# Modulated and low-rank feed-forward stages issued from one block instead of two

## The reference, cut to what matters

```python
# _L3_xattn_ref, its second half (the "modulated" stage)
scale_out, shift_out = jnp.split(c_t @ W_film_out + b_film_out, 2, axis=-1)
y = y * (1.0 + mod_gate * scale_out) + mod_gate * shift_out
xt = x_text + y
h = layernorm(xt, g_ffn, b_ffn)
h = jax.nn.gelu(h @ W1 + b1, approximate=False) @ W2 + b2      # 256 -> 1024 -> 256
xt = xt + h
return layernorm(xt, g_norm_out, b_norm_out)

# _L3_ffn_ref (the "low-rank" stage)
P = jnp.einsum('bsd,dr->bsr', x, U1)                           # 256 -> 64
H = jax.nn.gelu(jnp.einsum('bsr,rf->bsf', P, V1) + b1)         # 64 -> 1024
Q = jnp.einsum('bsf,fr->bsr', H, U2)                           # 1024 -> 64
return jnp.einsum('bsr,rd->bsd', Q, V2) + b2                   # 64 -> 256

x = x + _L3_xattn_ref(_layernorm(x, axis=-1), ...)
x = x + _L3_ffn_ref(_layernorm(x, axis=-1), ...)
```

## Time and profile before

| what | value |
|---|---|
| median of 3 runs (lowest to highest) | 4894.45 us (4890.16 to 4894.87) |
| the profiled execution's own time | 4895.16 us |
| its span, first to last instruction | 4893.4 us |
| mean granted TensorE clock, share of full | 0.962 |
| PE busy | 4476.2 us (91%) |
| DVE busy | 3200.3 us (65%) |
| ACT busy | 2002.0 us (41%) |
| POOL busy | 1820.1 us (37%) |

### The profile page before, as it was taken

How to read it: one execution, slowest core, us unless ns; L and a number is a source line. 1 busy time by engine, 2 the same in 40 slices (tenths; PEclk the granted TensorE clock), 3 DMA queues, 4 the chain that set the end, 5 groups by cost and what they waited for, 6 DMA issues and landing times. The chain is left out here.

```text
span 4893.4 us, 90645 instructions
## 1 busy us (share of the span) xinstructions
PE 4476.2 (91%) x31852; PEld 3480.9 (71%) x31852; DVE 3200.3 (65%) x9752; ACT 2002.0 (41%) x4152; POOL 1820.1 (37%) x2248
## 2 busy tenths in 40 slices
PE   7999869999995999699996999999999887999979
PEld 5666547778884888567765788888888645777856
DVE  5888789987552331278872888888888833444344
ACT  3555347754442331155552434434433342222234
POOL 2222145642553331255440333333333304665523
PEclk9999989999997999899998999999999988999989
DMA  4666512245313222222212010011100082222233
GB/s 115 155 154 150 122 60 78 71 139 157 58 55 68 71 70 70 59 72 68 76 52 79 27 28 28 29 31 33 28 28 24 18 277 96 88 85 85 73 114 106
DMA packets 332894, 391.33 MB, mean 80 GB/s; under 512 B 66485, under 2 KB 301467, under 8 KB 321691
## 3 DMA queue, kind: packets, MB, share of 16 engines
q1 hardware_dynamic: 319130, 360.28, 25.9%
q0 software_dynamic: 13312, 25.25, 2.1%
HBM read 296.33 MB, written 89.10 MB: 79 GB/s over the span
## 5 line engine op out<-in xcount | busy, mean ns | idle before, releaser
L2693 PE MATMUL fa_h<-fa_xnT,fa_w 128*128 128x256 f32 x2048 | 484.8, 382 | 0.0
L2705 PE MATMUL fa_y<-fa_w,fa_hT 128*128 128x256 f32 x2048 | 462.5, 379 | 0.0
L2693 PEld LDWEIGHTS fa_h<-fa_xnT,fa_w 128*128 128x128 f32 x2048 | 379.9, 190 | 81.9 <-issue 27.5
L2705 PEld LDWEIGHTS fa_y<-fa_w,fa_hT 128*128 128x128 f32 x2048 | 386.7, 190 | 65.1 <-issue 15.4
L2568 ACT ACTIVATE fa_hT<-fa_h,fa_b 128x256 f32<-128x256 f32 x512 | 214.5, 469 | 533.7 <-PE fa_h L2693 472.3
L516 DVE TENSOR_REDUCE a_mx<-a_score 128x16 f32<-128x1920 f32 x128 | 276.0, 2157 | 53.8 <-PE a_score L700 53.8
L3086 ACT ACTIVATE m_hT<-m_h,m_b 128x256 f32<-128x256 f32 x256 | 107.3, 470 | 363.2 <-PE m_h L3147 363.2
L1700 PE MATMUL r_h<-r_xnT,r_rw 128*128 128x256 f32 x1024 | 246.9, 389 | 0.0
L2007 ACT ACTIVATE e_hT<-e_h,e_b 128x256 f32<-128x256 f32 x256 | 107.3, 470 | 335.4 <-PE e_h L2061 335.4
L1846 POOL DMA_INDIRECT e_xg<-moe_rows,e_idx x64 | 128.6, 2009 | 307.9 <-issue 262.4
L3147 PE MATMUL m_h<-m_hnT,m_w 128*128 128x256 f32 x1024 | 235.7, 379 | 2.5 <-ACT m_hnT L3076 2.5
(11 more groups left out here) (463 smaller groups left out, 10842.1 us busy)
## 6 DMA issues: line engine op xcount, KB each, us to landing
a_floor<-a_lowest SPq DMA_DIRECT2D x64, 960.0 KB, 8.5
cv_toep<-kernels SPq DMA_DIRECT2D x16, 2048.0 KB, 9.3
x<-a_xo SPq DMA_DIRECT2D x96, 256.0 KB, 4.2
f_xb<-x SPq DMA_DIRECT2D x64, 256.0 KB, 2.8
f_xres<-x SPq DMA_DIRECT2D x64, 256.0 KB, 2.9
a_xb<-x SPq DMA_DIRECT2D x64, 256.0 KB, 3.3
e_w<-in_L_ffn_ew SPq DMA_DIRECT2D x16, 1024.0 KB, 7.5
a_cb<-in_ctx SPq DMA_DIRECT2D x96, 90.0 KB, 2.6
```

The costliest lines, as they stand in the source:

```text
L2693: last = pe.matmul(h_ps[j % 2][:, c, :], w1[:, e, k, f:f + P], xnT[it.p][:, k, :], start=k == 0, stop=k == KD - 1)
L2705: last = pe.matmul(bank[:, t * D:(t + 1) * D], hT[e % 2][:, k, t * P:(t + 1) * P], w2[:, e, k, :], start=k == 0, stop=k == KE - 1)
```

## The change

The two stages are put in one block. Each function now returns lists of steps (`Program`) in place of running them, and the new `modulated_to_low_rank` runs both with `run_parts`: the modulated part starts at slot 0, the low-rank part at slot 32. So the slots 32 to 40 hold the last batches of the one and the first of the other. The steps, their lags and their order within a part stay as they were.

What is new beside the form:
- The low-rank part's SP list begins 16 slots early (`-EARLY`), which puts its weight transfers at slot 16 of the modulated part. Its first load of `x` is issued in slot 31.
- `load` waits for the modulated store of the same batch.
- `f_hT` (the 1024-wide hidden values, two buffers) lies in the first eight batches of `xin`, which the modulated part has read by then; the first two batches' gelu waits for `mixed`.
- The PSUM banks are shared. The first use of each by the low-rank part waits for the last use by the modulated part (`values`, `film`, `turned`, `hidden`, `summed`).
- There is one `end_all` for both stages, behind the last store of the program. It clears 67 semaphores. Before, 40 were cleared between the stages and 28 at the end.

```diff
-def modulated_feed_forward(nc, const, src, dst, xin, rows_text, at_all, ctx, w):
+def modulated_feed_forward(nc, const, src, dst, xin, rows_text, at_all, ctx, w, first, area):
...
-    st = Stage(nc, "m3", [const["apart"]])
+    st = Stage(nc, "m3", [const["apart"]], area)
...
-            pipeline(pe, B, DEPTH, [(6, up(0)), (2, film_values), (6, up(1)), (6, up(2)), (2, film_product), (6, up(3)), (5, turn_x), (7, down)])
-    st.end()
+        return Program([(6, up(0)), (2, film_values), (6, up(1)), (6, up(2)), (2, film_product), (6, up(3)), (5, turn_x), (7, down)], 2, start)
+    after = dict(values=(v_ready, B), film=(film_ready, 2 * B), turned=(hn_ready, B), hidden=(h_ready, KH * B), summed=(summed, SUM * B),
+                 mixed=(mixed, MIX * B), stored=stored)
+    return st, after, Part(first, B, DEPTH, sync, gpsimd, vector, scalar, tensor)
...
-    st = Stage(nc, "f3", [const["apart"]])
+    st = Stage(nc, "f3", area=area)
...
-    hT = [st.sb(f"hT{p}", [P, KH, S]) for p in two]
-    t_ps, p_ps, q_ps, y_ps = st.ps("t", [P, 512]), st.ps("p", [P, 512]), st.ps("q", [P, 512]), st.ps("y", [P, TL, D])
-    h_ps = [[st.ps(f"h{m}{half}", [P, 2, S]) for half in range(HALVES)] for m in range(QUADS)]
+    hT = [xin[:, 4 * p:4 * p + 4].rearrange("p b t d -> p (b t d)").rearrange("p (k s) -> p k s", s=S) for p in two]
+    h01, y_ps, p_ps, q_ps, h00, h10, h11, t_ps = (st.ps(n, [P, 512] if n in "tpq" else [P, 2, S]) for n in ("h01", "y", "p", "q", "h00", "h10", "h11", "t"))
+    h_ps = [[h00, h01], [h10, h11]]
...
+    EARLY = 16
...
+            sp.wait_ge(before["stored"][it.p], 16 * (it.h + 1))
             sp.dma_start(xb[it.at][:], src_v[it.i]).then_inc(x_in[it.at], 16)
...
-            load(It(0, 0, 0, B, 4))
-            pipeline(sp, B, DEPTH, [(-1, load), (4, load_residual), (7, store)], **FOUR)
+        return Program([(-1, load), (4, load_residual), (7, store)], 4, start, -EARLY, finish)
...
+                if it.i < 2 and m == 0:
+                    act.wait_ge(*before["mixed"])
...
+            if it.i == 0:
+                pe.wait_ge(*before["values"])
...
+                if it.i == 0 and m == 0:
+                    pe.wait_ge(*before["film"])
+                    pe.wait_ge(*before["turned"])
+                if it.i == 0 and m == 1:
+                    pe.wait_ge(*before["hidden"])
...
+            if it.i == 0:
+                pe.wait_ge(*before["summed"])
...
+def modulated_to_low_rank(nc, const, src, dst, out, xin, rows_text, at_all, ctx, wm, wl):
+    area = Area((nc.sbuf_base, SBUF_END))
+    m3, m3_after, modulated = modulated_feed_forward(nc, const, src, dst, xin, rows_text, at_all, ctx, wm, 0, area)
+    f3, low_rank = low_rank_feed_forward(nc, const, dst, out, wl, xin, B, area, m3_after)
+    run_parts(nc, [modulated, low_rank])
+    end_all(nc, [m3, f3])
```

More of the change, by code:

```diff
@@ L2943, in keep_xt @@
[L2943 to L2967, removed]
+        def load(it):
+            if it.reused():
+                sp.wait_ge(xn_ready, it.i - 1)
+            apart(sp, const)
+            sp.dma_start(xb[it.p][:], src_v[it.i]).then_inc(x_in[it.p], 16)
@@ L2970, in _, with gpsimd, start @@
                 sp.wait_ge(xt_out[p], 16 * (B // 2))
-        @block.gpsimd
-        def _(pool):
+        return Program([(0, load), (1, load_context), (4, keep_xt), (6, load_xt), (7, load_residual), (9, store)], 2, start, finish=finish)
+    def gpsimd(pool):
+        def start():
             pool.wait_ge(weights, 192)
[L2976 to L3011, removed]
@@ new lines, in end @@
+        def end(it):
+            p = it.p
+            c = Chain(pool, ended, it.i, END)
+            pool.wait_ge(xn3_ready, it.i + 1)
+            if it.reused():
+                pool.wait_ge(stored[p], 16 * it.h)
+            c.add(pool.tensor_tensor(xo[p][:], xs[p][:], over(gout), ALU.mult))
+            c.wait()
+            c.add(pool.tensor_tensor(xo[p][:], xo[p][:], over(bout), ALU.add))
+            c.wait()
+            pool.wait_ge(r_in[p], 16 * (it.h + 1))
+            c.add(pool.tensor_tensor(xo[p][:], xo[p][:], xres[p][:], ALU.add))
@@ L3020, in _ @@
             dve.wait_ge(wready, 2)
[L3022 to L3068, removed]
-            act.wait_ge(weights, 192)
[L3071 to L3083, removed]
-                    for c in range(2):
-                        f = 2 * m + c
-                        act.activation(hT[it.p][:, f, :], h_ps[m % 2][:, c, :], ACT.Gelu, bias=b1[:, f:f + 1]).then_inc(h_ready, 1)
-                return step
-            def values_out(it):
-                act.wait_ge(v_done, it.i + 1)
-                if it.reused(1):
-                    act.wait_ge(f_done, it.i)
-                act.copy(vf[:], v_ps[0:SK, :]).then_inc(v_ready, 1)
@@ new lines, in norm_stats, with norm, film_out @@
+        def norm_stats(it):
+            dve.wait_ge(x_in[it.p], 16 * (it.h + 1))
+            layer_norm_stats(dve, Chain(dve, stats, it.i, 4), xb[it.p], stt[it.p], mv[it.p], const)
+        def norm(it):
+            dve.wait_ge(roots, 2 * it.i + 2)
+            if it.reused():
+                dve.wait_ge(mixed, MIX * (it.i - 1))
+            normalise(dve, xb[it.p], mv[it.p], rs[it.p], xn[it.p])[-1].then_inc(xn_ready, 1)
+        def film_out(it):
+            dve.wait_ge(f_done, it.i + 1)
+            if it.reused():
+                dve.wait_ge(mixed, MIX * (it.i - 1))
+            for t in range(TL):
+                dve.scalar_tensor_tensor(film[it.p][:, t, :], f_ps[t][:], gate[:, 0:1], bf[:], ALU.mult, ALU.add).then_inc(film_ready, 1)
@@ new lines, in last_norm, with scalar, hn_out, gelu @@
+        def last_norm(it):
+            dve.wait_ge(roots3, 2 * it.i + 2)
+            normalise(dve, xs[it.p], mv3[it.p], rs3[it.p], xs[it.p])[-1].then_inc(xn3_ready, 1)
+        return Program([(1, norm_stats), (5, xt_norm), (4, xt_stats), (2, norm), (2, film_out), (8, last_norm), (7, add_all)], 2, start)
+    def scalar(act):
+        def hn_out(it):
+            act.wait_ge(x_turned, it.i + 1)
+            if it.reused():
+                act.wait_ge(h_done, KH // 2 * (it.i - 1))
+            for k in range(KD):
+                last = act.activation(hnT[it.p][:, k, :], t_ps[:, k * S:(k + 1) * S], ACT.Identity, bias=bff[:, k:k + 1], scale=gf[:, k:k + 1])
+            last.then_inc(hn_ready, 1)
+        def gelu(m):
+            def step(it):
+                act.wait_ge(h_done, KH // 2 * it.i + m + 1)
+                if m == 0 and it.reused():
+                    act.wait_ge(y_done, it.i - 1)
+                for c in range(2):
+                    f = 2 * m + c
+                    act.activation(hT[it.p][:, f, :], h_ps[m % 2][:, c, :], ACT.Gelu, bias=b1[:, f:f + 1]).then_inc(h_ready, 1)
+            return step
+        def values_out(it):
+            act.wait_ge(v_done, it.i + 1)
+            if it.reused(1):
+                act.wait_ge(f_done, it.i)
+            act.copy(vf[:], v_ps[0:SK, :]).then_inc(v_ready, 1)
+        def start():
+            act.wait_ge(weights, 192)
@@ new lines, in down @@
+        def down(it):
+            pe.wait_ge(h_ready, KH * (it.i + 1))
+            if it.reused(1):
+                pe.wait_ge(summed, SUM * it.i)
+            for t in range(TL):
+                for k in range(KH):
+                    last = pe.matmul(y_ps[:, t, :], hT[it.p][:, k, t * P:(t + 1) * P], w2[:, k, :], start=k == 0, stop=k == KH - 1)
+            last.then_inc(y_done, 1)
+        return Program([(6, up(0)), (2, film_values), (6, up(1)), (6, up(2)), (2, film_product), (6, up(3)), (5, turn_x), (7, down)], 2, start)
@@ new lines, in scalar, with start, gelu, step @@
+    def scalar(act):
+        def start():
+            act.wait_ge(weights, 144)
+        def gelu(m):
+            def step(it):
+                act.wait_ge(h_done, QUADS * it.i + m + 1)
+                if it.i < 2 and m == 0:
+                    act.wait_ge(*before["mixed"])
+                if m == 0 and it.reused():
+                    act.wait_ge(q_done, it.i - 1)
+                for c in range(4):
+                    f = 4 * m + c
+                    act.activation(hT[it.p][:, f, :], h_ps[m][c % HALVES][:, c // HALVES, :], ACT.Gelu_apprx_tanh, bias=b1[:, f:f + 1]).then_inc(h_ready, 1)
+            return step
+        return Program([(5, gelu(m)) for m in range(QUADS)], 4, start)
```

389 lines of the change are left out of this document (213 added, 176 removed).

## The result

The changed kernel takes 4864.32 us (median of 4 runs, 4858.26 to 4867.37) against 4894.66 for the one before; the ratio is 0.9941, with a 95% interval of 0.9929 to 0.9953. It is faster by 30 us. The prediction was 4869.8, with a range of 4864.0 to 4876.5: right, but only 0.3 us inside its lower end. The profiled execution took 4864.60 us, its span 4862.9.

The account below looks back on a forecast made before the run. PE was taken to bound both stages, idle only in the seam's 26.7 us gap. Span 4893.4 - 28.2 (join) + 2.3 (clears) + 1.2 (clock) = 4868.7, adjusted from span to median time: 4869.8 us, range 4864 to 4876.5.

Parts of the forecast that it names:

- Part 1, the covered drain and the insertions: Slots 33 to 36: two turn_x and a narrow add 2.2 us on PE; weight transfers in slot 16 cost nothing.
- Part 2, the walk: Slots 37 to 40, followed step by step: up product of low-rank batch 4 starts 28.2 us earlier, despite 4.75 us waits.
- Part 2, the table load: Slot 37: a 1.28 us table load on ACT ahead of the first hidden values makes PE wait 1.2 us.
- Part 3, the clears: End of kernel: 39 more semaphore clears behind the last store add 2.3 us, bounds 0 and 2.5.
- Part 4, the clock: At the join: waits lower PE's granted clock, costing 1.2 us, bounds 0 and 1.7, from the earlier join near 1030 us.
- The sum: Whole kernel: span 4893.4 - 28.2 + 2.3 + 1.2 = 4868.7 us, hence a time of 4869.8.
- The smooth join: Rival at the join: 3.55 us of waits and the 1.2 of clock vanish, 4865.0 us; chance 0.12.
- The delayed modulated slots: Rival in slots 33 to 36: low-rank DVE and POOL work delays the modulated chain, +6.4 us, 4876.2; chance 0.15.
- No overlap: Rival at the seam: a wait keeps first loads behind the last store, only the weights' 5.5 us go, 4889; chance 0.03.
- The order that does not recover: Rival in the low-rank stage: batches stay 1.44 us over the steady 6.46 for 28 batches, +40, 4910 us; chance 0.04.

Follow-up runs that it names:

- experiment 3: Changed kernel with the nine low-rank weight transfers issued in slot 31 in place of slot 16: 4920.28 us, ratio 0.9963 to the kernel before.
- experiment 2: Changed kernel with POOL's residual one slot earlier (lag 5 in place of 6): ratio 0.9947 to the kernel before.
- experiment 8: Kernel before, with ACT's wait for the low-rank weights moved behind its wait for the first hidden values: ratio 0.9995 to the unedited one.
- experiment 1: Changed kernel with the low-rank part starting nine slots later (slot 41 in place of 32), so nothing overlaps: ratio 0.9986 to the kernel before.

## Why the prediction was right, point by point

- **Part 1, the covered drain and the insertions.** Right. PE is busy 30.00 of 30 us from 4609 to 4639; two turn_x and one narrow cost 0.44 + 0.86 + 0.44 = 1.7 us by the starts of PE's records in the new timeline, where I had 2.2. The weights cost nothing where the change issues them, in slot 16: from the first up product to the last film product PE took 481.6 and 480.8 us in the two profiles of the changed kernel and 480.8 before. But the reason that I gave, free time on SP, isn't the whole condition: they must have landed by slot 31, where PE itself waits for them (experiment 3). The walk has no such wait.
- **Part 2, the walk.** Right in the mechanism of all three waits; experiment 2 removes the one whose cause was named and only that. Together the waits are 3.10 us where I had 3.55.
- **Part 2, the table load.** Wrong: I put its 1.28 us, a wait of 1.2 on PE, into slot 37. It ran in the idle time before the data. Which wait a load carries is set by the order of the waits ahead of it; experiment 8 shows that by moving the load in the old kernel.
- **Part 3, the clears.** Right: 2.3 us, measured both ways (2.2 and 2.3).
- **Part 4, the clock.** Wrong: I took 1.2 us from the kernel's earlier join. From slot 33 on the granted clock stayed at the 2.4 GHz level in all nine profiles of overlapped kernels; in the changed kernel PE was busy 32.90 of 36 us. The page that I weighed against the row (the Trainium skill, TensorE: Matmul & The Clock Gate, "Loop structure matters more than you think") gave the better forecast: the trace agrees that copies out between products left the clock full (1.00 with waits of up to 1.73 us), and in experiment 3 a wait of 6.35 us for a transfer was followed by 0.50. Why the clock fell in the row that misled me is open. PE's busy time in the row alone, 2.39 of 4 us, doesn't explain it, for the changed kernel has a stretch as thin at full clock; what differs, untested as a cause, is that the 4 us ahead of that row were thin too. First the changed kernel's stretch:

```profile
4666.00:4670.00 4.00, 2.27 (x21) 1.50 (x17) 3.15 (x9) 2.58 (x8) 1.94 (x4) 1.00 0.19 66
```

The row ahead of it in the kernel before:

```profile
1024.00:1028.00 4.00, 1.87 (x17) 1.37 (x14) 3.66 (x2) 3.97 (x3) 0.61 (x1) 1.00 0.01 2
```

- **The sum.** Predicted for the seam: 28.2 - 2.3 - 1.2 = 24.7. Measured in S: 27.7. The difference of 3.0 is 1.2 (clock), 1.2 (table load), 0.45 (waits), and 0.15 left over: the insertions were 0.46 cheaper, the other steps together 0.3 dearer. The total was forecast 5.5 us too high: these 3.0, the 2.8 ahead of the join, which the forecast has no term for, less 0.3 for how far the profiled run lay from the median. That the range still held the time, by 0.3 us, is in part luck: the table load had no bound of its own and the 2.8 us no term.
- **The 2.8 us ahead of the join** need not be the edit's. In the profile of before the windows of the modulated stage's fill show half clock until its end (columns as above):

```profile
4074.00:4083.00 9.00, 7.52 (x8) 2.27 (x8) 4.79 (x12) 0.58 (x1) 7.45 (x9) 0.54 0.20 65
4083.00:4092.00 9.00, 8.12 (x12) 3.15 (x12) 6.54 (x15) 0.58 (x1) 5.58 (x7) 0.51 0.22 71
```

In that of after the full clock comes back at 4083:

```profile
4074.00:4083.00 9.00, 6.70 (x8) 1.97 (x8) 5.68 (x12) 0.58 (x1) 7.86 (x9) 0.62 0.25 77
4083.00:4092.00 9.00, 6.39 (x20) 3.27 (x20) 7.07 (x17) 3.24 (x5) 5.58 (x7) 1.00 0.27 88
```

The instructions there are the same. The fill took 29.5 us before and 25.5 after, but 29.4, 29.7, 29.1, 28.6 in other profiles of the merged block and 25.3 to 26.3 in the rest of them. So the merged block shows both. The kernel before shows only the long one, 29.5 in its own profile and in that of experiment 8, so whether the edit makes the short one more frequent stays open, and so does why the clock rises sooner in some runs.
- **The rivals.** The smooth join is refuted by the three waits, though its figure (4865.0) is near the result: right number, wrong reason. The delayed modulated slots: refuted, PE was busy 60.00 of 60 us from 4571 to 4631. No overlap: refuted by the timeline, and built as experiment 1. The order that does not recover: the steady batch is 6.46 us again from up(4) on.

## What to carry to other kernels

Where two pipelined stages meet at a barrier, the cost is the drain of the first, the fill of the second and the clears between; issuing both from one sequence of slots hides the first two, but moves the clears to where they are fully exposed, unless they are given to an idle queue. Two conditions go with it. What the new stage waits for at its start (here its weights) must have landed before its first slot, or each engine's wait for it stops the old stage: that cost 9 to 10 us here. And in the overlapped slots look on each engine for a late piece of the old stage that stands ahead of an early piece of the new one: moving one such piece by a slot bought back 1.8 us. To measure, compare a stretch that begins at a fixed instruction ahead of the change: it resolved terms of 0.8 to 2.3 us where whole times scatter by 10 us and more. But make sure that it begins ahead of everything the edit moves, and look at the whole times all the same: S showed no difference for the late weights, while the whole time was some 8 to 10 us longer.

## What the runs showed of the hardware that I had not expected

- A table load (1.283 us in every row) starts when the waits that it carries itself are met, and not with the gelu that it serves: at 4682.4 in one version of the old kernel and at 4673.7 in the other, with only the order of two waits changed.
- Three waits of up to 1.73 us within 20 us left the clock at its full level; after one of 6.35 us it was 0.50 over the next 4 us (experiment 3). In the fill of the modulated stage, with equal work, it stood at 0.51 in one profile and at 1.00 in another over the same 9 us, and the fill took 29.5 and 25.5 us, a difference of 4 us: more than most of the terms argued about here.
